# Local attention layers: norms spread as bf16 pieces, feed-forward products from f16 halves

## The reference

```python
h = _layernorm(x) * (1 + ca) + sa
x = x + ga * attn(h)                 # causal, 16 heads of 64, S = 512
h = _layernorm(x) * (1 + cb) + sb
x = x + gb * ffn(h)                  # here six further layers:
for i in range(6):
    x = attn_layer(shift_tokens(x), Wqkv[i], q_scale[i], k_scale[i], Wo[i]) + x
    x = ffn_layer(shift_tokens(x), ln_g[i], ln_b[i], W1[i], b1[i], W2[i], b2[i]) + x
```

## Time and profile before

| | |
|---|---|
| median of 3 runs | 3942.01 us |
| span of the profiled execution | 3944.5 us |
| TensorE busy (matmul) | 3691.1 us, 94% |
| VectorE busy | 2985.9 us, 76% |
| ScalarE busy | 2392.9 us, 61% |
| GpSimd busy | 2310.3 us, 59% |
| chain that ended last | TensorE 66%, issue 5%, DMA 4%, ScalarE 3% |

### The profile page before, as it was taken

One profiled execution on the slowest core, in us unless ns is written; L12 is line 12 of the kernel. 1 busy time (PEld: TensorE's weight loads), 2 busy tenths in 40 slices (PEclk: granted clock), 3 DMA queues, 4 the chain that ended last, 5 costly groups with the idle time before them and its releaser, 6 DMA issues.

```text
span 3944.5 us, 165118 instructions
## 1 busy us (share of the span) xinstructions
PE 3691.1 (94%) x73780; PEld 2146.6 (54%) x73780; DVE 2985.9 (76%) x3451; ACT 2392.9 (61%) x2931; POOL 2310.3 (59%) x1892
## 2 busy tenths in 40 slices
PE   7999998799999999999999999999999999999996
PEld 4666665455555555555555455555555555555553
DVE  7888886677777777777777677777777777777774
ACT  6777776455656655566555565555565656666652
POOL 4555654666655666656666565656565655666651
PEclk9999999899999999999999999999999999999998
DMA  1000001444444444445354444444444444444442
GB/s 59 5 5 7 5 5 39 106 100 111 101 101 104 108 108 104 101 95 123 89 121 95 97 103 108 108 107 96 109 112 109 101 101 103 110 103 106 101 101 77
DMA packets 162073, 349.17 MB, mean 89 GB/s; under 512 B 32606, under 2 KB 41948, under 8 KB 155100
## 3 DMA queue, kind: packets, MB, share of 16 engines
q1 hardware_dynamic: 161372, 338.62, 37.4%
HBM read 24.54 MB, written 4.19 MB: 7 GB/s over the span
## 4 chain that ended last, share of the span: by engine, by line
PE 66%; issue 5%; DMA 4%; ACT 3%; SPq 2%; DVE 2%; POOL 1%; ACTq 0%; DVEq 0%; POOLq 0%
PE psB L677 32%; PE psA L677 26%; DMA vev<-vo 3%; PE psA L732 3%; PE psB L758 2%; PE psB L732 2%; ACT pb L1015 1%; PE psA L758 1%; ACT vo L1007 1%; SPq L502 1%; SPq L486 1%; SPq L504 1%; DMA kf<-h 1%; DVE h L1253 0%; ACT sq L985 0%
## 5 line engine op out<-in xcount | busy, mean ns | idle before, releaser
L1354 POOL TENSOR_TENSOR sq<-sq 128x512 f32<-128x512 f32 x384 | 490.1, 1295 | 492.6 <-ACT sq L985 492.3
L1349 POOL TENSOR_TENSOR h<-h,ts 128x512 f32<-128x512 f32 x384 | 490.3, 1277 | 211.1 <-DVE ts L1245 211.1
L1329 POOL TENSOR_TENSOR pt<-wk,pt 128x256 f16<-128x256 f32 (+3 forms) x256 | 368.0, 1453 | 286.6 <-ACT pt L908 196.9
L1350 POOL TENSOR_TENSOR h<-h,ts 128x512 f32<-128x512 f32 x384 | 489.6, 1275 | 0.0
L985 ACT ACTIVATE sq<-psA 128x1024 f32<-128x1024 f32 x240 | 245.7, 1024 | 168.3 <-PE psA L677 168.2
L1237 DVE TENSOR_TENSOR h<-psA,t_rot 128x1024 f32<-128x1024 f32 x240 | 293.0, 1221 | 38.1 <-ACT sq L985 17.3
L677 PE MATMUL psB<-vev,ptb 64*32 64x65 f32 x9216 | 244.4, 225 | 59.0 <-ACT pb L1015 35.2
L1245 DVE TENSOR_TENSOR ts<-psA,t_rot 128x1024 f32<-128x1024 f32 x240 | 291.6, 1215 | 3.1 <-POOL h L1350 3.1
L677 PEld LDWEIGHTS psB<-vev,ptb 64*32 64x32 f32 x9216 | 194.7, 106 | 175.5 <-issue 103.3
L1364 POOL TENSOR_SCALAR f_a<-f_a 128x512 f32<-128x512 f32 x48 | 31.2, 650 | 401.6 <-DVE f_a L1293 401.6
L1253 DVE TENSOR_TENSOR h<-h,psB 128x1024 f32<-128x1024 f32 x192 | 229.5, 1217 | 42.4 <-PE psB L677 40.3
(11 more groups left out here) (343 smaller groups left out, 10637.5 us busy)
## 6 DMA issues: line engine op xcount, KB each, us to landing
qf<-h SPq DMA_DIRECT2D x768, 136.0 KB, 2.5
kf<-h SPq DMA_DIRECT2D x768, 136.0 KB
vev<-vo SPq DMA_DIRECT2D x192, 260.0 KB, 4.1
vev<-vo SPq DMA_DIRECT2D x192, 227.5 KB, 4.6
stage<-wqk SPq DMA_DIRECT2D x12, 512.0 KB, 4.6
stage<-wvl SPq DMA_DIRECT2D x12, 256.0 KB, 5.3
stage<-wof SPq DMA_DIRECT2D x6, 512.0 KB, 5.1
xb<-xt SPq DMA_DIRECT2D x8, 256.0 KB, 8.1
```

The costliest lines, as they stand in the source:

```text
L1329: e.tensor_tensor(pt[g][pr][:, :, 1, o:o + w], wk[(slot_of(s)[0] - 1) % SLOTS][:, :, 0:w], pt[g][pr][:, :, 0, o:o + w], ALU.subtract).then ...
L1349: e.tensor_tensor(halves_of(h, 0), halves_of(h, 0), t[1], ALU.subtract)
L1350: e.tensor_tensor(halves_of(h, 1), halves_of(h, 1), t[0], ALU.add).then_inc(ended["ad"])
L1354: e.tensor_tensor(sqb[c][:, 0, :], sqb[c][:, 0, :], sqb[c][:, 1, :], ALU.add).then_inc(ended["qa"])
```

## The change

- The inverse norms, f32 in n_a, are spread by bf16 matmuls. Rows 0 to 3 of each 32 keep the value, rows 4 to 7 the value less its bf16 rounding, rows 8 to 11 that less its own rounding; the 0/1 matrix `spread` sums the three. New steps: ca (ScalarE: n_c = n_a in bf16), cs (VectorE: n_a += less * n_c), cb and ct the same again, with the result in n_b (bf16). bc waits for ct.
- f and fo multiply f16 halves, three products for each f32 one. New steps: fh (ScalarE), fl (GpSimd) split f_c; gh (ScalarE, three times), gl (GpSimd, three times) split f_g. The weights are split by VectorE once a layer: `first_halves` (with gain and a factor 8) after the last fm of a layer, `second_halves` after the last fr.
- b2 becomes a row of w2, against a row of ones in f_gh; fr scales by 1/64 in its place.
- The next layer's w1 and w2 are fetched at half-step 8 of a layer, once the split of this layer's is done and lb has read w1r.
- All five orders are new; mx waits for all four sc of its group, and a few steps are put first in their walks.
- The constant tiles: `spread` moves to the bf16 tile, `less` is added; the scratch of the dynamic DMAs is set to 1024.

```diff
     heads = (q // W == np.arange(W)[None, :] % 4) * 1.0
-    spread = (q % W == k // W) * 1.0
-    mats = np.concatenate([np.eye(128), np.eye(128) - 1.0 / 128, np.full((128, 128), 1.0 / 128), spread, heads], 1)
+    spread = ((q % W < 12) & (q % 4 == k // W)) * 1.0
+    masks = np.concatenate([np.eye(128)] + lsel + [np.tile(np.eye(2 * W), (2, 1)), spread] + parts, 1)
...
 TENSOR = (
-    "vp00:A ot00:B pj10:A pj11:B sc100:B tp01:A sc101 sc102 sc103 pj13:A pj12:A ng10 pv011:B pv010:B ss1:B "
-    "sc110:A tp10:B sc111 sc112 ot01:B sc113 f1:A ng11 pv100:B f2:B f0:B pv101:A bc11:A vp10:B bc10:A tp11:B "
-    "pj01:B+1 vp11:A pv111:B ot10:A pj00:A+1 pv110:B pj02:B+1 vp01:A+1 pj03:A+1 ot11:B sc000:A+1 sc001+1 sc002+1 "
-    "fo:B ss0:A+1 sc003+1 op:B ng00+1 sc010:B+1 sc011+1 sc012+1 la:A+1 sc013+1 tp00:A+1 bc00:B+1 ng01+1 pv001:A+1 "
-    "lb:A+1 pv000:B+1 bc01:B+1 "
+    "pv110:B bc11:A pv111:B pj00:B+1 f0:B pj02:A+1 pj03:A+1 ot11:B sc000:B+1 sc002+1 sc003+1 sc001+1 ss0:A+1 op:B "
+    "ng00+1 vp01:A+1 sc010:A+1 tp00:B+1 sc012+1 sc011+1 sc013+1 la:A+1 pv001:B+1 ng01+1 pv000:B+1 bc00:B+1 tp01:A+1 "
+    "lb:A+1 bc01:B+1 pj11:A+1 ot00:B+1 pj10:B+1 pv010:A+1 vp11:A+1 pv011:A+1 sc100:B+1 sc102+1 sc101+1 sc103+1 "
+    "pj12:A+1 pj13:B+1 ng10+1 fo:A ot01:B+1 tp10:A+1 ss1:A+1 pv101:A+1 f1:A+1 sc110:B+1 sc111+1 sc113+1 sc112+1 "
+    "f2:A+1 pj01:B+2 ng11+1 pv100:A+1 vp10:A+1 ot10:A+1 tp11:B+1 bc10:B+1 vp00:A+2 "
 )
 SCALAR = (
-    "ve11 oe10 sq00+1 sq02+1 ve01+1 sq03+1 oe11 nr0+1 ns0+1 ex00+1 lq+1 lw+1 tb1+1 te00+1 ex01+1 lr+1 oe00+1 "
-    "sq10+1 ve00+1 sq11+1 te01+1 sq13+1 sq12+1 ex10+1 xh+2 nr1+1 ns1+1 oe01+1 te10+1 oh ex11+1 ge1+1 wh0+1 ge2+1 "
-    "ge0+1 ve10+1 te11+1 sq01+2 wh1+1 "
+    "fh oe01 te10 nr1 ns1 ge1 ge2 ca1 sq01+1 ex11 cb1 oe10 ve10 gh2 te11 ve00+1 sq00+1 ge0 sq02+1 xh+1 wh1 sq03+1 "
+    "oe11 gh1 nr0+1 ns0+1 ex00+1 gh0 ve01+1 ca0+1 oh te00+1 cb0+1 lq+1 lw+1 ex01+1 te01+1 lr+1 tb1+1 sq11+1 sq10+1 "
+    "oe00+1 wh0+1 ve11+1 sq12+1 ex10+1 sq13+1 "
 )
 VECTOR = (
-    "tc01+1 ts01+1 nm111 ol10 tc00+1 ts00+1 nm110 tc02+1 wl1 ts02+1 tc03+1 ts03+1 ol11 mx00+1 fr rs mx01+1 bm00+1 "
-    "bm01+1 nm001+1 nm000+1 bm02+1 ln+1 bm03+1 ol00+1 tc10+1 ts10+1 tc11+1 ts11+1 mx10+1 tc13+1 nm011+1 ts13+1 "
-    "nm010+1 tc12+1 ts12+1 mx11+1 ol01+1 nm100+1 fm1+1 wl0+1 fm2+1 ow nm101+1 fm0+1 bm12+1 bm13+1 bm10+1 bm11+1 "
+    "cs0+1 mx01+1 wl1 ct0+1 nm001+1 nm000+1 bm01+1 bm00+1 bm02+1 bm03+1 ln+1 tc11+1 ts11+1 nm010+1 ol00+1 tc10+1 "
+    "ts10+1 mx10+1 nm011+1 tc12+1 ts12+1 fr tc13+1 ts13+1 wl0+1 ol01+1 nm101+1 mx11+1 fm1+1 fm2+1 cs1+1 nm100+1 "
+    "tc01+2 ts01+2 ct1+1 ol10+1 bm11+1 bm10+1 nm110+1 nm111+1 bm12+1 bm13+1 tc00+2 ow ts00+2 fm0+1 tc02+2 ts02+2 "
+    "ol11+1 mx00+2 tc03+2 ts03+2 rs+1 "
 )
 GPSIMD = (
-    "lx qa10 ad10 qa11 qa13 qa12 ad11 xl+1 ad13 nw1 ad12 qa01+1 ad01+1 ad00+1 qa00+1 qa03+1 qa02+1 ad03+1 nw0+1 "
-    "ad02+1 "
+    "ad02+1 xl+1 gl0 gl2 lx+1 qa10+1 ad11+1 ad10+1 qa11+1 qa12+1 qa13+1 fl+1 ad12+1 nw1+1 ad01+2 qa01+2 ad13+1 qa00+2 "
+    "qa02+2 qa03+2 ad00+2 gl1+1 nw0+2 ad03+2 "
 )
 SYNC = (
-    "dm00+1 dm01+1 dm02+1 st0 st1 dm03+1 vd0+1 dm10+1 dm11+1 dm13+1 dm12+1 vd1+1 "
+    "st0 dm13 dm01+1 dm00+1 dm03+1 st1 dm02+1 vd0+1 dm11+1 dm10+1 dm12+1 vd1+1 "
 )
...
+        scalar_walk = with_first(scalar_walk, ("xh", 0), ("wh", -2), ("tb", 0))
+        vector_walk = with_first(vector_walk, ("wl", -2))
+        gpsimd_walk = with_first(gpsimd_walk, ("xl", 0))
+        sync_walk = with_first(sync_walk, ("st", -2))
...
-                if u == 2 and li:
-                    e.wait_ge(*all_done("f", *((NB * li - 1, j) for j in range(3))))
-                    e.wait_ge(*done("fo", NB * li - 1))
-                    feed_of(e, li)
+                if u == 8 and li + 1 < L:
+                    e.wait_ge(*done("lb", NB * li))
+                    e.wait_ge(s_w1s, li + 1)
...
-                    e.wait_ge(*done("nw", v))
+                    e.wait_ge(*done("ct", v))
                     for x in range(2):
                         rows = slice(64 * k + 32 * x, 64 * k + 32 * x + 32)
-                        p = mm(o[:, 512 * x:512 * x + 512], spread[rows, :], n_a[rows, :], tile_position=(64 * k + 32 * x, 0))
+                        p = mm(o[:, 512 * x:512 * x + 512], spread[rows, :], n_b[rows, :], tile_position=(64 * k + 32 * x, 0))
...
-                    e.wait_ge(*done("lx", v))
                     e.wait_ge(s_w1s, v // NB + 1)
+                    e.wait_ge(*done("fl", v))
                     for x in range(2):
-                        p = mm(o[0:n, 512 * x:512 * x + 512], w1r[:, FF * x + 128 * j:FF * x + 128 * j + n], f_c[:, :])
+                        at = FF * x + 128 * j
+                        oy = o[0:n, 512 * x:512 * x + 512]
+                        mm(oy, w1s[1][:, at:at + n], f_ch[:, :], True, False)
+                        mm(oy, w1s[0][:, at:at + n], f_cl[:, :], False, False)
+                        p = mm(oy, w1s[0][:, at:at + n], f_ch[:, :], False, True)
                     p.then_inc(ended["f"])
                 elif kind == "fo":
                     o = take(s)
-                    e.wait_ge(*all_done("fm", *((v, j) for j in range(3))))
-                    e.wait_ge(s_w2, 48 * (v // NB + 1))
+                    e.wait_ge(s_w2s, v // NB + 1)
+                    e.wait_ge(*all_done("gl", *((v, j) for j in range(3))))
                     for j in range(3):
-                        n = FP[j]
-                        p = mm(o[:, 0:512], w2r[0:n, j, :], f_g[j][0:n, :], j == 0, j == 2)
+                        n = FK[j]
+                        mm(o[:, 0:512], w2s[1][0:n, j, :], f_gh[j][0:n, :], j == 0, False)
+                        mm(o[:, 0:512], w2s[0][0:n, j, :], f_gl[j][0:n, :], False, False)
+                        p = mm(o[:, 0:512], w2s[0][0:n, j, :], f_gh[j][0:n, :], False, j == 2)
                     p.then_inc(ended["fo"])
 
         def scalar(e):
             e.preload_act_table_set("natural_log_exp_and_others")
-            e.wait_ge(s_ct, 16)
+            e.wait_ge(s_cin, 16)
             e.activation(t_ct[:, 1, :], t_ct[:, 0, :], ACT.Exp, scale=-1.0).then_inc(s_actc)
...
-                    if v:
-                        e.wait_ge(*all_done("bc", (v - 1, 0), (v - 1, 1)))
                     e.activation(n_a[:, :], n_r[:, :], ACT.Square, scale=0.5 ** 0.5).then_inc(ended["ns"])
+                elif kind == "ca":
+                    e.wait_ge(*done("nw", v))
+                    e.activation(n_c[:, :], n_a[:, :], ACT.Copy).then_inc(ended["ca"])
+                elif kind == "cb":
+                    e.wait_ge(*done("cs", v))
+                    e.activation(n_c[:, :], n_a[:, :], ACT.Copy).then_inc(ended["cb"])
                 elif kind == "ve":
...
+                        e.wait_ge(*done("gl", v - 1, j))
+                    e.activation(f_g[j][0:n, :], psum(("f", v, j))[0:n, 512:1024], ACT.Gelu, bias=b1s[0:n, 3 + j:4 + j],
+                                 scale=1.0 / WF).then_inc(ended["ge"])
+                elif kind == "fh":
+                    if v:
+                        e.wait_ge(*all_done("f", *((v - 1, j) for j in range(3))))
+                    e.wait_ge(*done("lx", v))
+                    e.activation(f_ch[:, :], f_c[:, :], ACT.Copy).then_inc(ended["fh"])
+                elif kind == "gh":
+                    j = s[2]
+                    n = FP[j]
+                    if v:
                         e.wait_ge(*done("fo", v - 1))
-                    e.activation(f_g[j][0:n, :], psum(("f", v, j))[0:n, 512:1024], ACT.Gelu, bias=b1s[0:n, 3 + j:4 + j]
-                                 ).then_inc(ended["ge"])
+                    e.wait_ge(*done("fm", v, j))
+                    e.activation(f_gh[j][0:n, :], f_g[j][0:n, :], ACT.Copy).then_inc(ended["gh"])
 
         def vector(e):
...
+        def first_halves(e, li):
+
+            e.wait_ge(s_w1, 16 * (li + 1))
+            g = t_gs[:, li:li + 1]
+            e.tensor_scalar(w1s[0][:, :], w1r[:, :], g, None, ALU.mult).then_inc(s_w1h)
+            e.wait_ge(s_w1h, li + 1)
+            e.scalar_tensor_tensor(out=w1s[1][:, :], in0=w1r[:, :], scalar=g, in1=w1s[0][:, :], op0=ALU.mult,
+                                   op1=ALU.subtract).then_inc(s_w1s)
+
+        def second_halves(e, li):
+
+            e.wait_ge(s_w2, 48 * (li + 1))
+            for j in range(3):
+                n = FK[j]
+                e.tensor_scalar(w2s[0][0:n, j, :], w2r[0:n, j, :], WF, None, ALU.mult).then_inc(s_w2h)
+            e.wait_ge(s_w2h, 3 * li + 3)
+            for j in range(3):
+                n = FK[j]
+                p = e.scalar_tensor_tensor(out=w2s[1][0:n, j, :], in0=w2r[0:n, j, :], scalar=WF, in1=w2s[0][0:n, j, :],
+                                           op0=ALU.mult, op1=ALU.subtract)
+            p.then_inc(s_w2s)
+
...
+            e.memset(f_gh[2][64:128, :], WF).then_inc(s_ones)
+            e.memset(f_gl[2][64:128, :], 0.0).then_inc(s_ones)
```

(38 more changed lines are left out.)

71 lines of the change are left out of this document (41 added, 30 removed).

## The result

The changed kernel takes 3995.65 us (median of 4 runs, 3993.7 to 4004.1) where the kernel before takes 3941.8: a ratio of 1.0143, 95% interval 1.0128 to 1.0157, so 1.4% slower (54 us between the medians, 56 by the ratio). The forecast was 3736 us, range 3645 to 3850.

A forecast was written before the change was run, and what follows sets the result against it. TensorE's own work was taken to set the pace: 3944.5 - 262 (saving) + 10 (weights' split) + 36 (norm chain) + 10 (collisions) = 3738.5, so 3736 us against the runs' median, range 3645 to 3850.

The forecast's parts named there:

- TensorE's own work sets the pace: Local layers: TensorE needs 63.6 of 66.7 us per iteration and bounds the kernel; VectorE, 50.4, comes next.
- TensorE's saving: 16-bit matmuls save 146 us in bc, 76 in f, 40 in fo: 262 in all, bounds 215 to 280.
- 3944.5 - 262: The sum: TensorE's whole saving comes off the span, then 10, 36 and 10 us are added, giving 3738.5.
- The prediction's own sign of being wrong: One of its signs of error: TensorE's idle time per iteration grows by over 2 us.
- the rings have slack in the new order like that before: Argument for rival (a), whole saving or more: shortest buffer distances some 0.8 to 1.4 us in both orders; chance 0.25.
- VectorE's added work: Four cs and ct operations per iteration at 1.1 us each, 4.4 us; VectorE goes from 50.4 to 54.8.
- The weights' halves: VectorE's split once a layer: about 2 us net, 5 times beyond the first, counted as +10 us.
- The norm's chain: Inverse norms' four new links: half 1's bc up to 1.5 us late per iteration, half counted, +36 us; half 0 fits.
- Rival (c): Pieces' chain in ScalarE's queue makes it slower once each half's bc is over 2.7 us late; 4019 at 3.5; chance 0.06.
- 4 table loads: ScalarE per iteration: loads rise from 2 to 4, +2.6 us, within 47.6 us total; nothing on the sum.
- forecast 47: GpSimd per iteration: fl and three gl add 4.5 us, waiting about 2, making 47 us; room too.
- Rival (b): VectorE becomes the bound at 57.4 us per iteration, in-order queues waiting for each other: 3755 to 3840; chance 0.24.

The follow-up runs named there:

- k14: The kernel before with bm on half its columns, about 200 us less VectorE work in a run; 3931.4 us, ratio 0.9990.
- k9: TensorE's saving in the kernel before's orders: one bf16 norm piece, high halves replacing low ones, no added steps but the weights' split; 3815.7 us, ratio 0.9688.
- k9b: The same computation as k9, in the new orders less the eight new step kinds; 3920.3 us, ratio 0.9945.
- k1: The kernel before with the five new orders, their waits, mid-layer fetch and a second w1r/w2r buffer, no new step kinds; 4004.8 us, ratio 1.0164.
- k3: The changed kernel with cs and ct on 8 of their 512 columns, places and handovers kept; 3980.2 us, ratio 1.0093.
- k16: The changed kernel with the weights' halves made once, before the first local layer, for all layers; 3968.9 us, ratio 1.0057.
- k2: The changed kernel with the gelu replaced by the identity, so no table is loaded; 3999.5 us, ratio 1.0157.
- k4: The whole change in the kernel before's orders, new steps inserted and one first spread moved; 4038.6 us, ratio 1.0250.
- k20: k9 with the feed-forward's halves whole and a second bf16 norm piece made by ca and cs; 3980.8 us, ratio 1.0106.

## Why the prediction was wrong, point by point

**What bounds the kernel.** "TensorE's own work sets the pace" was right for the kernel before, as far as runs tell: 140 us less of VectorE in the stage bring nothing (k14), and TensorE's saving brings something (k9).

**TensorE's saving.** Nearly right in size: by the page the busy time fell by 230 us in k9 and by 210 in after, forecast 262 in 215 to 280. The bc pair takes 0.40 us from start to next start in the median (0.32 at the fast end), forecast 0.30 in 0.22 to 0.53; f takes 1.33 for 1.29, fo 1.945 for 1.94. That matmuls in different row groups run concurrently, a few ns apart, as the Trainium skill has it (TensorE: Matmul & The Clock Gate, Part 3, The mechanism), the trace agrees: the two of a pair start 4 ns apart in the median. A whole step did not come down to the 0.22 that the prediction made of it. Per iteration TensorE's busy time fell by 4.6 us and not 5.5; a part of the difference is the clock, below.

**The step that failed is the sum: "3944.5 - 262".** It takes the saving one to one, in the rate of an engine that is 94% busy. k9 shows 123 us of 262. What I missed, as I now read it: the list of each engine waits for the others, and TensorE's idle time of 3 us per iteration was low because TensorE was late at its meetings with them. An engine that gets shorter arrives early, in k9 at VectorE's ts and GpSimd's sq, and waits there. The prediction's own sign of being wrong, idle time that grows by over 2 us per iteration, came: it grew by 5.5. The miss divides as follows (in us, from the ratios): forecast 206 faster, measured 56 slower, 262 in all. 139 of the saving doesn't arrive in the old orders (k9; up to 34 of it is the weights' split, which k9 has, and some 30 is that the busy time fell by 230); 101 is the new orders on top (k9 to k9b); 78 is the added steps where I had 56 (k9b to after), 22 more. This is one way through the runs, and by another the parts have other sizes: the orders cost 65 without the saving (k1) and 101 after it.

**The orders priced at nothing.** I wrote of the new orders only that "the rings have slack in the new order like that before", and priced them nowhere but in the norm's chain. They cost 65 us alone. I had looked at the distance between a PSUM buffer's last write and its next use, on TensorE, and not at where VectorE stands when TensorE asks: the waits for ts, 4 in the earlier trace rows, are 36 in k1's row. How the 65 divide between such waits and the stalls is open.

**VectorE's added work.** Its size was right: 54.7 us per iteration, forecast 54.8; cs 0.89 and ct 1.09 a piece, forecast 1.1. ct took 0.74 at least and 1.74 at most. Where it began first, GpSimd's operation behind it took 1.71 for its usual 1.27 (VectorE's row, then GpSimd's):

```profile
2042.32 0.74 DVE L1311 SCALAR_TENSOR_TENSOR n_b<-n_c,t_mats,n_a 128x512 bf16<-128x512 bf16 x1
```

```profile
2042.48 1.71 POOL L1410 TENSOR_TENSOR h<-h,ts 128x512 f32<-128x512 f32 x1 [4.96 <-DVE ts L1294]
```

The Trainium skill has the rule that whoever starts first keeps the other out (SBUF — State Buffer, Who interferes with whom). The trace agrees: the 48 ct that began before GpSimd's operation took 0.74 us, the 47 that began into one 1.63 in the median. That VectorE's added work lay beside TensorE's work, at no cost in the sum, was wrong: k3 gets 20 us back for a half of it. I named what is queued behind ca and cb, but not what is queued behind cs: VectorE waits 1.1 us for it and its list waits too.

**The weights' halves.** "About 2 us net" a layer is a mis-sized term: 7.6 us, 7.0 net, of which w2h has 3.5. I had scaled 0.56 us down by columns; GpSimd's company made 0.22 us into 1.16. They cost 34 us (k16), forecast 10.

**The norm's chain.** Forecast 1.5 us late in one half. TensorE's waits for n_b are 20.1 us in 2400, 0.6 per iteration. (The bare chain of 10.0 also leaves out the 0.55 us from ScalarE's end at 2016.88 to GpSimd's start at 2017.43 in the earlier trace rows.) Rival (c), its turning point at 2.7 us, was not what made the kernel slower. **ScalarE** with its 4 table loads has 46.2 us per iteration, forecast 47.6, and they are harmless (k2). **GpSimd** has 46.4, forecast 47. **Rival (b)**, VectorE as the bound, had a part of the mechanism, in-order lists that wait for each other, but it asked for 57.4 us of VectorE's work. With 54.7, an in-order list and waits in it the period is already 65.3 in mid-layer.

**Clock.** The granted clock of the stage is 0.97 (before 0.99). Here, in stretches of after, it fell when TensorE had been busy for 0.65 of 3 us, and rose again after it had been busy throughout:

```profile
2908.00:2911.00 3.00, 0.65 (x57) 0.48 (x46) 0.73 (x1) 0.04 (x1) 3.00 (x3) 1.00 0.66 148
2911.00:2914.00 3.00, 3.00 (x20) 1.24 (x21) 2.03 (x3) 0.66 (x1) 1.84 (x2) 0.67 1.09 224
2914.00:2917.00 3.00, 3.00 (x12) 1.17 (x11) 2.35 (x2) 1.21 (x2) 1.27 (x1) 0.76 0.66 172
2917.00:2920.00 3.00, 3.00 (x25) 2.26 (x27) 1.85 (x3) 2.64 (x5) 1.82 (x2) 1.00 0.01 2
```

Between 700 and 3900 us the granted clock is at its lower level, 1.2 for 2.4 GHz, for 157 us in after, 88 in before, 110 in k1, 164 in k4 and 106 in k20. That is at most (157 - 88) / 2 = 35 us of after's loss. No run takes the clock away by itself, so this is a bound and no more; k20 loses 42 us, of which the clock can be at most (106 - 88) / 2 = 9.

**What stays open**: which of the moves in the five new orders costs the 65 us, and whether it is by the waits behind VectorE, by the stalls or by both; and what holds back the rest of the saving in k9. The weights' splits are not in k1 and so no part of its 65 us.

## What to carry to other kernels

Before a saving on the busiest engine is taken one to one, ask at each meeting with the next engine how early that engine is now (the idle time before its operations, by releaser): what the saving has beyond that, the busiest engine can lose again as waits. Here 123 of 262 us arrived. A step inserted into an in-order list can cost its duration and its own wait, and all that stands behind it is later by both. Orders and durations belong together: try the changed operations in the old order with the new steps taken out (k9) and the new order with the old operations (k1) first; these two runs held most of the answer.

## What the hardware showed beyond that

TensorE has stalls of 0.9 to 3.2 us in which it waits for no semaphore: in after 54 between 700 and 3900 us, 96 us in all (before 23, 30 us). From one to the next lies a whole multiple of 256 of its instructions, its sequencer's counted in, for all 54, and 45 of them stand in the scores, among the shortest instructions. The page has a queue for instructions:

```profile
q8 instruction: 588, 9.63, 1.0%
```

These are packets of 16 KB, about one for each 256 of TensorE's instructions. All 54 stalls end 1.2 to 1.7 us after such a packet ended; a moment picked at random lies 3.3 us behind one in the median. That fits with a fetch of instructions that comes late; no run tried it by itself.

On GpSimd the scaling of a bf16 tile in place took 1.56 us and that of an f32 tile 0.62.
